# The last part of a fused convolution, attention and expert kernel laid out anew, with its last gate and pooling in halves

## The reference

```python
x = x + conv(group_norm(x))        # upsample by 2, 12 x 12 filter, leaky ReLU, 12 x 12 filter, downsample
t = t + attention(layer_norm(t))   # per image, causal, one head of width 32
t = t + experts(layer_norm(t))
# experts, per image: 16 experts choose 8 tokens each
logits = u @ gate_w.T + gate_b
probs = softmax(logits, axis=1)             # over the 1024 tokens
topv, topi = top_k(probs.T, 8)
pooled = sum over the 8 of topv * u[topi]   # one vector of 32 per image and expert
h = gelu([pooled, 1] @ weight1)             # 128 hidden, exact gelu
out = [h, 1] @ weight2
outputs[topi] += out * topv                 # scattered back to the tokens
```

## Time and profile before

| | us |
|---|---|
| median of 3 runs | 368.54 |
| lowest and highest | 368.35, 369.02 |
| profiled execution | 368.35 |
| its span, first to last instruction | 366.5 |
| PE busy | 327.2 (89%) |
| DVE busy | 260.1 (71%) |
| ACT busy | 183.9 (50%) |
| POOL busy | 128.8 (35%) |

### The profile page before, as it was taken

The page is one execution under the profiler, slowest core; times in us unless marked ns, Lnnn a source line. Parts: engine busy times, 40 slices in busy tenths (PEclk is TensorE's granted clock), DMA queues, the critical chain, the costliest instruction groups (busy, mean ns, idle before and its releaser), DMA issues.

```text
span 366.5 us, 8381 instructions
## 1 busy us (share of the span) xinstructions
PE 327.2 (89%) x3362; PEld 249.3 (68%) x3362; DVE 260.1 (71%) x523; ACT 183.9 (50%) x251; POOL 128.8 (35%) x96
## 2 busy tenths in 40 slices
PE   2289998799999999999899999999996986979985
PEld 1168886587777878786678787777774544546774
DVE  2679779957757877869686876776988786454632
ACT  1043355446557574757663755576564547440500
POOL 6134535332444337554211557312235400351000
PEclk9999999999999999999999999999999899995655
DMA  4910100001011010101000101011021100100122
GB/s 125 204 36 3 26 19 16 16 16 31 16 18 26 5 32 2 31 4 32 15 16 2 31 15 17 17 16 26 7 58 32 31 2 18 28 2 29 57 75 69
DMA packets 35906, 11.16 MB, mean 30 GB/s; under 512 B 24431, under 2 KB 35741, under 8 KB 35869
## 3 DMA queue, kind: packets, MB, share of 16 engines
q1 hardware_dynamic: 33152, 9.98, 11.3%
q10 hardware_dynamic: 2717, 0.66, 1.2%
HBM read 5.72 MB, written 4.21 MB: 27 GB/s over the span
## 4 chain that ended last, share of the span: by engine, by line
PE 77%; DVE 10%; DMA 5%; issue 3%; ACT 2%; POOL 1%; ACTq 1%; SPq 0%; DVEq 0%; POOLq 0%
PE psB L892 14%; PE psA L892 13%; PE psB L1025 9%; PE psB L1005 8%; PE psA L990 7%; PE psA L1070 4%; PE psA L882 3%; PE psA L1048 3%; PE psB L1039 3%; DVE negmax L757 2%; PE psA L993 2%; PE psA L983 2%; PE psA L1032 2%; PE psB L1008 2%; PE psB L977 2%
## 5 line engine op out<-in xcount | busy, mean ns | idle before, releaser
L757 DVE TENSOR_REDUCE negmax<-psA 128x1 f32<-128x512 f32 (+7 forms) x128 | 90.5, 751 | 32.2 <-PE psA L993 31.6
L587 ACT ACTIVATE Pp<-psB 128x1024 f32<-128x1024 f32 (+1 forms) x80 | 73.6, 937 | 35.3 <-PE psB L1008 30.7
L892 PE MATMUL psB<-xin,UU 128*128 128x224 f16 (+1 forms) x480 | 56.4, 277 | 0.1
L892 PE MATMUL psA<-y,DD 128*128 128x224 f16 (+1 forms) x480 | 55.1, 273 | 0.0
L990 PE MATMUL psA<-zK,yQ 128*128 128x512 f16 (+1 forms) x192 | 47.8, 332 | 6.0 <-DVE uT L775 2.4
L892 PEld LDWEIGHTS psB<-xin,UU 128*128 128x128 f16 x480 | 47.0, 99 | 7.9 <-DVE xin L698 0.5
L1005 PE MATMUL psB<-yQ,zK 128*128 128x512 f16 (+1 forms) x192 | 47.3, 330 | 3.7 <-DMA yQ<-rows 2.4
L892 PEld LDWEIGHTS psA<-y,DD 128*128 128x128 f16 x480 | 46.7, 98 | 5.5
L477 POOL TENSOR_TENSOR zrstd<-zrstd,power 128x8 f32<-128x8 f32 x16 | 27.2, 1698 | 53.9 <-DVE zrstd L735 53.9
L557 ACT ACTIVATE y<-psB 128x1024 f16<-128x1024 f32 x16 | 16.4, 1023 | 44.8 <-PE psB L892 44.8
L499 POOL TENSOR_TENSOR y<-y 128x1024 f16<-128x1024 f32 x16 | 34.1, 2132 | 9.8 <-ACT y L560 9.8
(11 more groups left out here) (158 smaller groups left out, 504.5 us busy)
## 6 DMA issues: line engine op xcount, KB each, us to landing
x_all<-in_x_dram SPq DMA_DIRECT2D x4, 512.0 KB, 3.9
normalised_tokens<-z SPq DMA_DIRECT2D x16, 128.0 KB, 1.8
zV<-normalised_tokens SPq DMA_DIRECT2D x64, 32.0 KB, 2.1
out_dram<-x_all SPq DMA_DIRECT2D x8, 256.0 KB, 2.3
yQ<-rows SPq DMA_DIRECT2D x32, 2.0 KB
Pp<-filter_tables ACTq DMA_DIRECT2D x4, 121.9 KB, 3.7
w_halves<-y SPq DMA_DIRECT2D x12, 32.0 KB, 1.8
cst<-shape_constants SPq DMA_DIRECT2D x1, 326.5 KB, 4.3
```

What stands on the lines that cost most here:

```text
L587: nc.scalar.activation(Pp[:, n % 2, UOFF[e[2]]:UOFF[e[2]] + N], slot(e)[:, 0:N], ACT.Exp).then_inc(b_drained, 1)
L757: ins = nc.vector.tensor_reduce(negmax[:, n % 2, m - 1:m], s[:, at:at + P * m], X, ALU.max, negate=True)
L892: ins = nc.tensor.matmul(within(out_cols, -shift), m, within(v, shift), start=i == 0, stop=i == len(matrices) - 1)
```

## The change

- `proj`, `mean` and `dev` of images 12 to 15 get orders of their own. `proj` of image 14 comes before `pv` of image 15 and, as that of image 15, takes one bank; ACT's squaring becomes an event, `square`, placed apart from `mean`, for the last group. The last group's scaling of `u` is done by DVE for all three parts (`scale`), POOL only takes the roots, and `urstd` has a place for each part.
- `wT` goes to ring B in all four groups: ACT copies it. That also changes which banks the events behind it get, in both rings.
- For the last group, `uT` is copied in two halves and the first half of the logits begins after the first; ACT's scaling and DVE's masking in `route` are in two halves; `wT` has two banks, its halves are transposed and copied one by one, and `pool` begins its first four tiles after the first copy.
- `scatter(1,1)` moves from between `uT` and `logits` to behind `select`; `scatter(0,0)` moves behind `pool`, and `scatter(0,1)` behind `hidden(1)`.
- Fillers: three fewer in `pv` of image 15 (7, not 10), one more before `turned`, none before `scatter(1,0)` (3 before).

```diff
+LATE = ((G - 1, 0), (G - 1, 1), LAST_IMAGE)
...

-LAST = [("proj", G - 1, 2), ("hidden", 0), ("mean", G - 1, 2), ("experts", 0), ("dev", G - 1, 2), ("turned", 0), ("scale", G - 1, 2),
-        ("scatter", 1, 0), ("uT", G - 1), ("scatter", 1, 1), ("logit_max", G - 1), ("logits", G - 1), ("select", G - 1), ("scatter", 2, 0),
-        ("logit_exp", G - 1), ("route", G - 1), ("scatter", 2, 1), ("scatter", 0, 0), ("wT", G - 1), ("pool", G - 1), ("scatter", 0, 1),
-        ("hidden", 1), ("experts", 1), ("turned", 1), ("scatter", G - 1, 0), ("scatter", G - 1, 1)]
-
-
-FILL = {("experts", 0): 5, ("turned", 0): 2, ("scatter", 1, 0): 3}
-FILL_PV = (0, 5, 2, 1, 2)
-FILL_HOME = ("proj", G - 1, 1)
+LAST = [("prob", B - 1, 0), ("pv", B - 2), ("prob", B - 1, 1), ("wT", G - 2), ("prob", B - 1, 2), ("mean", G - 1, 0), ("pool", G - 2),
+        ("prob", B - 1, 3), ("prob", B - 1, 4), ("square", G - 1, 0), ("proj", G - 1, 1), ("mean", G - 1, 1), ("dev", G - 1, 0),
+        ("pv", B - 1), ("hidden", 0), ("square", G - 1, 1), ("proj", G - 1, 2), ("mean", G - 1, 2), ("square", G - 1, 2), ("dev", G - 1, 1),
+        ("scale", G - 1, 0), ("experts", 0), ("dev", G - 1, 2), ("scale", G - 1, 1), ("turned", 0), ("scale", G - 1, 2), ("scatter", 1, 0),
+        ("uT", G - 1), ("logit_max", G - 1), ("logits", G - 1), ("select", G - 1), ("scatter", 1, 1), ("logit_exp", G - 1),
+        ("route", G - 1), ("scatter", 2, 0), ("scatter", 2, 1), ("wT", G - 1), ("pool", G - 1), ("scatter", 0, 0), ("hidden", 1), ("scatter", 0, 1), ("experts", 1),
+        ("turned", 1), ("scatter", G - 1, 0), ("scatter", G - 1, 1)]
+
+
+FILL = {("experts", 0): 5, ("turned", 0): 3}
+FILL_PV = (0, 5, 2, 0, 0)
+FILL_HOME = ("proj", G - 1, 2)


 def schedule():
     events = list(FIRST)
-    for t in range(-9, B + 6):
+    for t in range(-9, B - 1):
         for event in STEP:
             e = event(t)
...
-ON_A = ("xT", "small", "dnT", "gn_mean", "gn_var", "proj", "score", "uT", "shift", "down", "wT", "pool", "yQ",
+ON_A = ("xT", "small", "dnT", "gn_mean", "gn_var", "proj", "score", "uT", "shift", "down", "pool", "yQ",
...
+ON_B = ("up", "prob", "logits", "pv", "tok", "zK", "hidden", "wT")
 A = {e: n for n, e in enumerate(e for e in EVENTS if e[0] in ON_A)}
 BU = {e: n for n, e in enumerate(e for e in EVENTS if e[0] in ON_B)}
 BANKS = 4
...
-        size = 1 if e[0] in ONE_BANK or (e[0] in ("score", "prob") and e[2] == NU - 1) else 2
+        size = 1 if e[0] in ONE_BANK and e != ("wT", G - 1) or e[0] == "proj" and e[1] == G - 1 and e[2] > 0 or (e[0] in ("score", "prob") and e[2] == NU - 1) else 2
...
-        urstd = sb("urstd", [P, 2 * KT])
+        urstd = sb("urstd", [P, 3, 2 * KT])
...
+        def halves_of(n):
+
+            return ((0, BANK), (BANK, S)) if n == G - 1 else ((0, S),)
...
                     first, last = span_of(*e[1:])
                     pool.wait_ge(t2_var, 2 * g + e[2] + 1)
-                    inverse_root(urstd[:, 0:KT * (last - first)], KT * (last - first)).then_inc(t2_rstd, 1)
-                    if e[1:] != LAST_IMAGE:
+                    inverse_root(urstd[:, e[2], 0:KT * (last - first)], KT * (last - first)).then_inc(t2_rstd, 1)
+                    if e[1:] not in LATE:
                         pool.wait_ge(t2_rstd, 2 * g + e[2] + 1)
                         v = part_of_u(first, last)
-                        nc.gpsimd.tensor_tensor(v, v, per_token(urstd[:, :], last - first), ALU.mult).then_inc(u_ready, 1)
+                        nc.gpsimd.tensor_tensor(v, v, per_token(urstd[:, e[2], :], last - first), ALU.mult).then_inc(u_ready, 1)
...
-                elif name == "mean":
+                elif name == "square" or name == "mean" and n < G - 1:
                     m = 2 * n + e[2]
-                    act.wait_ge(t2_centred, m + 1)
+                    if e[1:] == LAST_IMAGE:
+                        act.wait_ge(last_centred, 1)
+                    else:
+                        act.wait_ge(t2_centred, m + 1)
...
-                    nc.scalar.activation(probs[:, :], probs[:, :], ACT.Copy, scale=inverse[:, 0:1]).then_inc(p_scaled, 1)
+                    for lo, hi in halves_of(n):
+                        nc.scalar.activation(probs[:, lo:hi], probs[:, lo:hi], ACT.Copy, scale=inverse[:, 0:1]).then_inc(p_scaled, 1)
...
+                elif name == "wT":
+                    if n >= 1:
+                        act.wait_ge(a_filled, A["pool", n - 1] + 1)
+                    to = wT[:, :, :].rearrange("p k n -> p (k n)")
+                    if n < G - 1:
+                        nc.scalar.activation(to, slot(e)[:, 0:KT * GE], ACT.Copy).then_inc(b_drained, 1)
+                    else:
+                        half = R * GE
+                        act.wait_ge(wT_half, 1)
+                        nc.scalar.activation(to[:, 0:half], slot(e)[:, 0:half], ACT.Copy).then_inc(wT_copied, 1)
+                        act.wait_ge(b_filled, BU[e] + 1)
+                        nc.scalar.activation(to[:, half:2 * half], slot(e)[:, BANK:BANK + half], ACT.Copy).then_inc(b_drained, 1)
...
-                if e in A and name != "yQ":
+                if e == ("uT", G - 1):
+                    dve.wait_ge(uT_half, 1)
+                elif e in A and name != "yQ":
                     dve.wait_ge(a_filled, A[e] + 1)
...
-                    if m >= 1:
-                        dve.wait_ge(u_ready, m)
-                    squares, spread = uss[:, 0:KT * (last - first)], urstd[:, 0:KT * (last - first)]
+                    if n >= 1 and e[1:] != LAST_IMAGE:
+                        dve.wait_ge(u_ready, m - 1)
+                    squares, spread = uss[:, 0:KT * (last - first)], urstd[:, e[2], 0:KT * (last - first)]
                     link(nc.vector.tensor_reduce(squares, sq_u[:, 0:BC * (last - first)].rearrange("p (n c) -> p n c", c=C), X, ALU.add))
                     nc.vector.tensor_scalar(spread, squares, 1.0 / C, EPS, ALU.mult, ALU.add).then_inc(t2_var, 1)
                 elif name == "scale":
                     first, last = span_of(*e[1:])
-                    dve.wait_ge(t2_rstd, 2 * G + 1)
+                    dve.wait_ge(t2_rstd, 2 * n + e[2] + 1)
                     v = part_of_u(first, last)
-                    nc.vector.tensor_tensor(v, v, per_token(urstd[:, :], last - first), ALU.mult).then_inc(u_ready, 1)
+                    nc.vector.tensor_tensor(v, v, per_token(urstd[:, e[2], :], last - first), ALU.mult).then_inc(u_ready, 1)
                 elif name == "uT":
-                    nc.vector.tensor_copy(uT[:, :].rearrange("p (a q r) -> p a r q", a=2, r=R),
-                                          s.rearrange("p (a r q) -> p a r q", a=2, r=R)).then_inc(a_drained, 1)
+                    to, v = uT[:, :].rearrange("p (a q r) -> p a r q", a=2, r=R), s.rearrange("p (a r q) -> p a r q", a=2, r=R)
+                    if n < G - 1:
+                        nc.vector.tensor_copy(to, v).then_inc(a_drained, 1)
+                    else:
+                        nc.vector.tensor_copy(to[:, 0], v[:, 0]).then_inc(uT_copied, 1)
+                        dve.wait_ge(a_filled, A[e] + 1)
+                        nc.vector.tensor_copy(to[:, 1], v[:, 1]).then_inc(a_drained, 1)
...
-                    dve.wait_ge(p_scaled, n + 1)
-                    nc.vector.scalar_tensor_tensor(out=xF_all[0:GE, n, :], in0=rest[:, :], scalar=NEG, in1=probs[:, :],
-                                                   op0=ALU.is_equal, op1=ALU.mult).then_inc(route_ready, 1)
+                    for i, (lo, hi) in enumerate(halves_of(n)):
+                        dve.wait_ge(p_scaled, n + 1 + i)
+                        nc.vector.scalar_tensor_tensor(out=xF_all[0:GE, n, lo:hi], in0=rest[:, lo:hi], scalar=NEG, in1=probs[:, lo:hi],
+                                                       op0=ALU.is_equal, op1=ALU.mult).then_inc(route_ready if hi == S else route_half, 1)
...
+            def turn(s, src, idn, n=P, first=0, last=KT, half=None):
+
+                for k in range(first, last):
                     ins = nc.tensor.transpose(s[:, n * k:n * k + n], src(k), idn)
+                    if half is not None and k == R - 1:
+                        ins.then_inc(half, 1)
                 return ins
...
-                    ins = turn(s, lambda k: u[:, k, :], ident)
+                    ins = turn(s, lambda k: u[:, k, :], ident, half=uT_half if n == G - 1 else None)
                 elif name == "logits":
-                    pe.wait_ge(a_drained, A["uT", n] + 1)
                     for i in range(2):
+                        if n == G - 1 and i == 0:
+                            pe.wait_ge(uT_copied, 1)
+                        else:
+                            pe.wait_ge(a_drained, A["uT", n] + 1)
                         ins = nc.tensor.matmul(s[0:GE, BANK * i:BANK * i + BANK], gateT[:, :, :], uT[:, BANK * i:BANK * i + BANK], start=True, stop=True)
                         if i == 0:
                             ins.then_inc(logits_half, 1)
```

(30 more changed lines are left out.)

9 lines of the change are left out of this document (3 added, 6 removed).

## The result

The changed kernel takes 366.29 us (median of 4 runs, 365.60 to 366.71) beside 368.45 us for the kernel before: ratio 0.9939, 95% interval 0.9916 to 0.9962. The forecast was 367.2 us, its range 365.3 to 369.0. The profiled execution took 366.71 us with a span of 364.8 us (before: 368.35 and 366.5).

A forecast was written before the change was run, and what follows sets the result against it. The chain was taken to be mostly PE, with the tail a fixed list of PE work with few gaps. 2.38 - 2.5 - 1.95 - 0.85 + 1.75 = -1.17 us from 368.35 gave 367.2 us, range 365.3 to 369.0.

The forecast's parts named there:

- Part 1: Main part: wT on ring B re-pairs buffers, three new PE waits and one lost, nothing given back: +2.38 us.
- The three waits: PE ahead of prob(7,2) (+0.99, released by ACT), score(10,3) and score(11,3) (+1.10 each, released by DVE).
- The wait of 0.81: PE's wait ahead of score(12,1) for proj(2,0) goes, as it gets down(14)'s bank: -0.81 us.
- rival A: Main part: no low-clock stretch after the 283.44 wait (365.5 us), or Part 1's stalls half covered (366.0); chance 0.20.
- Part 2: Up to the last uT: proj(3,2) reaches DVE 3.3 us sooner, scatter(1,0) follows turned(0)'s spreading, uT starts earlier: -2.5 us.
- Rival C: Part 2 gives nothing: DVE's chain to turned(0) is late, 1.2 us equals the old kernel, all lost 369.7; chance 0.15.
- Part 3: From uT to the logits: scatter(1,1) moved behind, uT copied in halves, 2.2 us instead of 4.14: -1.95 us.
- Part 4: Logits to pool: halving wT fills the 0.88 gap ahead of pool, halving the gate buys nothing: -0.85 us.
- A tie of 0.1 us: Ahead of wT: PE's scatters end at 347.26, route's DVE product at 347.15, so halving gate and selection buys nothing.
- Part 5: After pool: scatter(0,1) takes 2.16 between hidden(1) and experts(1), where PE waited only 0.41: +1.75 us.
- rival B: The clock falls once more, at the 308.76 wait: one stretch 368.9 us, two in a row 370.6; chance 0.15.
- My price of 1.7 us for a fall: Main part: 3.3 us of PE at 0.50 clock after a long wait loses half of that, 1.7 us.

The follow-up runs named there:

- e5: Kernel before, with 11 empty matmuls ahead of zK(15) and 9 ahead of prob(15,0), in PE's two long waits: 366.56 us, ratio 0.9953.
- e9: Changed kernel, with 11 empty matmuls ahead of zK(15) and 9 ahead of prob(15,0), in PE's two long waits: 364.71 us, ratio 0.9891.
- e2: Changed kernel with turned(0) placed ahead of scale(3,1) in the list: 365.2 us, ratio 0.9905.
- e6: Changed kernel with the last group's route (gate and selection) in one piece, wT's halves kept: 367.41 us, ratio 0.9967.
- e7: Changed kernel with the last wT copied in one piece, route's halves kept: 366.4 us, ratio 0.9952.
- e8: Changed kernel with wT of groups 0 to 2 on ring A, turned(0) ahead of scale(3,1), and both long PE waits filled: 362.69 us, ratio 0.9842.
- e10: e8 with square(3,1), dev(3,1) ahead of pv(15) and experts(0), dev(3,2), turned(0) ahead of scale(3,0): 361.9 us, ratio 0.9813.
- e11: Changed kernel, unaltered, measured a second time: 365.64 us, ratio 0.9918.
- e3: Changed kernel with 9 empty matmuls ahead of prob(15,0) only: 365.63 us, ratio 0.9916.
- e4: Changed kernel with the last scatters placed as in the kernel before: 366.58 us, ratio 0.9938.
- e1: Changed kernel with wT of groups 0 to 2 back on ring A, copied by DVE; only the last wT on ring B: 364.69 us, ratio 0.9899.

## Why the prediction was right, and where it wasn't

The time lies in the range and 0.9 us below the number. e5 and e9 have both waits filled and no fall before 326 us, so they give each part without those falls (distances in the table):

| part | forecast | e5 to e9 | how |
|---|---|---|---|
| 1 rings | +2.38 | +1.66 | zK(15): 97.96 - 96.30 |
| 2 to uT | -2.50 | -2.48 | uT: -0.82, less part 1 |
| 3 uT to logits | -1.95 | -1.78 | 2.36 against 4.14 |
| 4 logits to pool | -0.85 | -2.07 | 9.57 against 11.64 |
| 5 after pool | +1.75 | +1.72 | 15.50 against 13.78 |
| sum | -1.17 | -2.95 | |

**Part 1: the right waits, too large a sum.** The three waits stand where they were foretold, with releasers as foretold, and the rows behind them start 1.00, 1.10 and 1.04 us later (for 0.99, 1.10 and 1.10). The next products are pushed by 0.87, 1.05 and 1.04 us (pv(7), pv(8), pv(9) in before and after). The wait of 0.81 vanished. The step that failed is the sentence "I see nothing that gives it back". By pv(7) 0.13 us are given back already; pv(10) lost its wait of 0.20 on ACT as well (its delay is 0.98 less than pv(9)'s, not 0.81), wT(1)'s transposes, on the other ring now, came 0.20 sooner and pool(1) 0.10 sooner. Together some 0.7 of 2.4 us. These are small waits, below where I looked, in a stretch where each counts. The prediction had named the sign of it (waits "followed by a gap that shrinks"), and rival A had the mechanism in a larger size.

**Part 2 holds**, by its own path. proj(3,2) is taken up by DVE 3.6 us sooner once part 1 is taken off (324.03 - 187.65 = 136.38 in e9, 324.71 - 186.40 = 138.31 in e5, and 1.66 between them is part 1), for 3.3. scatter(1,0) starts right behind the spreading of turned(0) (330.48 + 0.67 = 331.15, PE at 331.30), which stands behind scale(3,1); e2 shows that this order is what counts in the changed kernel. No run takes the new order of `proj`, `mean` and `dev` back by itself, so this part is read from the timelines. They also show a piece that the prediction did not name. Before, the spreading was over well ahead of scatter(1,0), which stood behind three empty matmuls:

```profile
330.12 0.68 DVE L863 TENSOR_TENSOR obd<-psA,cst 64x128 f32<-64x128 f32 x3 [0.35 <-PE psA L1065]
...
330.02 1.46 PE L898 MATMUL psA<-ident_h 128*128 128x512 f16 x3
331.41 2.23 PE L1070 MATMUL psA<-obd,xF_all 64*128 64x128 f32 x8
```

With the 0.15 us that lie between spreading and scatter after, scatter(1,0) could have begun at 330.95: an estimate of 0.45 us for those fillers, which the changed kernel no longer has there.

Rival C, the chain late by a microsecond or more, did not come. The table load took its 1.28 us and the GELU came 1.30 us behind the load's start (324.38, 325.68), as in the earlier trace rows, so the further 1.38 us of drain that the Trainium skill states (ScalarE: Activation LUTs, "What ACT_TABLE_LOAD costs") was rightly left out of the sum.

**Part 3** was 0.17 us less than forecast: half a copy took 1.06 us for 1.0, and the wait for it 0.40 where 0.2 was allowed for all releases.

**Part 4** has three pieces. The gap ahead of pool: -0.80 for -0.85. The gate in halves, costed at nothing because PE's scatters hold it: -0.23 (e6). A tie of 0.1 us is no cover, since PE could otherwise begin beside the last scatter. And about -1.03 from the clock, which I did not forecast: from the logits to the wT transposes e9 takes 8.31 us and e5 9.58. The logits in e5, then in e9, and the stretch around them in the two:

```profile
335.93 3.65 PE L1039 MATMUL psB<-uT,gateT 128*64 128x512 f32 x4
...
334.58 2.68 PE L1073 MATMUL psB<-uT,gateT 128*64 128x512 f32 x4 [0.40 <-DVE uT L839]
```

```profile
328.30:341.80 13.50, 13.49 (x42) 8.71 (x41) 6.56 (x13) 2.34 (x5) 1.56 (x1) 0.55 0.13 39
...
328.30:341.80 13.50, 11.32 (x40) 8.77 (x40) 8.12 (x17) 4.27 (x8) 2.19 (x2) 0.75 0.07 19
```

0.97 of it is the logits' own row: full clock reaches into them in e9 (336.2 to 343.0 us) and not in e5 (340.5 to 343.9). It isn't safe to credit this to the change: e7 and e6 have the changed order here and take 9.34 and 9.57, with 3.64 and 3.65 for the logits, and e8 and e10, with both waits filled, take 9.34.

**Part 5** was off by 0.03. Parts 3 and 5 belong together: they are the same scatter, taken out of one gap and put into another, and come to -0.06 us. What the change gains lies in parts 2 and 4.

**The profiled executions.** From pv(6) to the last sum 176.08 before and 174.28 after, -1.80. The parts without the clock give 1.66 - 2.48 - 1.78 - 1.04 + 1.72 = -1.92, where -1.17 was forecast; part 1 makes 0.72 of that difference, and parts 3 and 4 nearly cancel. The rest is the clock: before paid 1.12 us up to uT (146.51 against e5's 145.39), 0.97 for its fall at 284 and the rest in the matmuls from 327 us on, after paid 1.74 (146.31 against e9's 144.57), 1.62 of it for the fall at 311, and got 0.47 of the 1.03 back behind the logits: -1.12 + 1.74 - 0.47 = +0.15, sum -1.77. So in the first profile rival A (no fall at 284) and rival B (a fall at the other wait) came at once and nearly cancelled. That the profiled time came out 0.5 us from the forecast (366.71 for 367.2) is in part luck: the forecast had counted on the fall at 284 staying and none at 311. Both were right as events and wrong as alternatives: they change with the execution, not with the kernel. My price of 1.7 us for a fall was too high at 284 (0.97 in before against e5; 0.69 in e2 against e11, both by pv(14)) and right at 311 (1.6 to 1.7), where pv(14) and the whole path to image 15 lie under it.

**What stays open.** What decides in which execution the clock falls. The changed main part with neither or one wait filled was profiled seven times: a fall at 285 or 286 us four times (e2, e3, e4, e6), at 311 once, none twice (e7, e11). With the old main part and no filling it came at 284 both times (before, e1). With both waits filled it came in none of four (e5, e8, e9, e10). Two of two is too few to say that the old order always falls. Of the timed runs only the mean granted clock is on record. It is 0.944 to 0.949 in the 29 runs of the kernel before that stand beside these experiments, 0.949 to 0.955 in e5's five, and 0.951 to 0.963 in e11's six. One stretch of 3.3 us at 0.50 makes about 0.005 of such a mean (an estimate: 3.3 / 2 / 366.5). That speaks for a fall in most runs of the old order, but the tail's clock moves the mean as well, so it isn't shown.

## What to carry to other kernels

Move only the event that gains from the other ring: a rotation that deals out buffers in the order of a list re-pairs every later event, and here the three groups that had nothing to win paid 1.7 us for the fourth. Compare traces from the last point ahead of the first difference, not from the span's start, and take the small waits of 0.1 to 0.2 us into the sum where an engine is busy nearly all the time. Fill the long waits of both kernels with empty matmuls before comparing them: that took away accidents of 0.7 to 1.6 us, where 1.9 us were to be measured. When an instruction only changes sides of a gap, price both sides before counting either.
